# Chunked ridge attention and an fp4 feed-forward on one core: three passes against one, and two ways to invert the same small matrices

## The reference, cut to what matters

```python
G = Kc.T @ Kc + RIDGE_EPS * I            # 64 x 64
W = jnp.linalg.solve(G, Kc.T @ Vc)
U = U0                                   # first RANK = 8 unit vectors
for _ in range(POWER_K):                 # 2 rounds
    U, _ = jnp.linalg.qr(W @ U)
Wr = U @ (U.T @ W)
S_new = DECAY_ALPHA * S + Wr
out = SCALE * (Qc @ S_new)
```

```python
h = _layernorm(x) * (1 + ca) + sa
x = x + ga * attention(h)
h = _layernorm(x) * (1 + cb) + sb
x = x + gb * fp4_linear(silu(fp4_linear(h, w_gate)) * fp4_linear(h, w_up), w_down)
```

## Time and profile before

| what | value |
|---|---|
| runs | 1950.42, 1954.88, 1956.24 us |
| profiled execution, span from first to last instruction | 1955.5 us |
| DVE busy | 1637.0 us (84%) |
| PE busy | 1111.4 us (57%) |
| ACT busy | 796.1 us (41%) |
| POOL busy | 120.1 us (6%) |
| DMA, mean over the span | 38 GB/s |

### The profile page before, as it was taken

The page is one execution under the profiler, slowest core; times in us unless marked ns, Lnnn a source line. Parts: engine busy times, 40 slices in busy tenths (PEclk is TensorE's granted clock), DMA queues, the critical chain, the costliest instruction groups (busy, mean ns, idle before and its releaser), DMA issues. The chain is left out here.

```text
span 1955.5 us, 54893 instructions
## 1 busy us (share of the span) xinstructions
PE 1111.4 (57%) x21470; PEld 912.4 (47%) x21470; DVE 1637.0 (84%) x5229; ACT 796.1 (41%) x1499; POOL 120.1 (6%) x119
## 2 busy tenths in 40 slices
PE   2438201891662876776486867377407717347876
PEld 1325101851552863575485456277306616235554
DVE  6865799699999489999939999976998970399997
ACT  3645100652541553673354465255406404124342
POOL 3530000000000002000001100000201000200000
PEclk6659655695895688898669889758758959579998
DMA  2551000000000002100000200000121110411220
GB/s 91 173 182 57 27 0 0 15 29 12 3 3 1 4 3 81 35 4 3 2 4 24 81 2 4 2 3 4 61 78 43 39 39 2 132 51 57 66 64 28
DMA packets 58236, 73.85 MB, mean 38 GB/s; under 512 B 4512, under 2 KB 32880, under 8 KB 57984
## 3 DMA queue, kind: packets, MB, share of 16 engines
q1 hardware_dynamic: 57984, 70.38, 11.4%
HBM read 44.61 MB, written 25.76 MB: 36 GB/s over the span
## 5 line engine op out<-in xcount | busy, mean ns | idle before, releaser
L1500 DVE TENSOR_TENSOR a_blocks<-a_blocks,a_outer 128x384 f32<-128x384 f32 (+3 forms) x1024 | 455.3, 487 | 0.0
L1494 DVE TENSOR_TENSOR a_outer<-a_blocks,a_scaled 128x128 f32<-128x128 f32 (+3 forms) x1024 | 440.7, 492 | 2.0 <-DVE a_blocks L1528 1.3
L1150 ACT ACTIVATE a_pair<-a_bank 32x512 f32<-32x512 f32 (+1 forms) x352 | 207.2, 592 | 205.6 <-PE a_bank L932 126.5
L932 PE MATMUL a_bank<-a_ident,a_blocks 128*128 128x128 f32 x256 | 46.8, 367 | 366.7 <-DVE a_blocks L1510 366.7
L1150 ACT ACTIVATE a_work<-a_bank 32x512 f32<-32x512 f32 (+1 forms) x224 | 130.7, 589 | 294.5 <-PE a_bank L932 222.9
L932 PEld LDWEIGHTS a_bank<-a_ident,a_blocks 128*128 128x128 f32 x256 | 45.3, 214 | 368.3 <-DVE a_blocks L1510 197.8
L883 PE MATMUL a_bank<-a_wk,a_cg 128*128 128x512 f32 x256 | 123.6, 630 | 11.5 <-issue 11.5
L951 PE MATMUL a_bank<-a_work,a_gram 64*32 64x32 f32 (+1 forms) x4096 | 105.8, 220 | 17.9 <-issue 14.7
L951 PEld LDWEIGHTS a_bank<-a_work,a_gram 64*32 64x32 f32 (+1 forms) x4096 | 98.6, 135 | 23.4 <-issue 21.4
L1150 ACT ACTIVATE a_xb<-a_bank 128x512 f32<-128x512 f32 x112 | 63.4, 596 | 112.4 <-PE a_bank L1056 63.8
L1432 POOL TENSOR_TENSOR a_xc<-a_xc,a_ga 128x512 f32<-128x512 f32 x16 | 23.2, 1453 | 1358.2 <-ACTq L1155 1311.6
(11 more groups left out here) (212 smaller groups left out, 2625.5 us busy)
## 6 DMA issues: line engine op xcount, KB each, us to landing
f_x<-in_L_attn_x SPq DMA_DIRECT2D x16, 256.0 KB, 3.2
s_xnt<-f_xt SPq DMA_DIRECT2D x16, 256.0 KB, 2.1
s_c<-f_cm SPq DMA_DIRECT2D x16, 256.0 KB, 2.3
s_base<-f_base SPq DMA_DIRECT2D x16, 256.0 KB, 2.8
a_cg<-s_c SPq DMA_DIRECT2D x16, 256.0 KB, 2.7
a_cc<-s_c SPq DMA_DIRECT2D x16, 256.0 KB, 3.6
a_xnt<-s_xnt SPq DMA_DIRECT2D x16, 256.0 KB, 3.7
a_base_in<-s_base SPq DMA_DIRECT2D x16, 256.0 KB, 2.7
```

Of the source, the lines that this page charges most:

```text
L932: last = nc.tensor.transpose(bank[:, i * P:(i + 1) * P], rows_[:, :, 4 * jb + i], ident[:])
L1150: nc.scalar.activation(out, view, ACT.Copy, scale=scale).then_inc(emptied, 1)
L1494: made[a] = ch.inc(V.tensor_tensor(outer[a // KEPT], bcast(factor, 3, HB - a), bcast(scaled[:, :, a:HB], 2, KEPT), ALU.mult))
L1500: differences = ch.inc(V.tensor_tensor(strip, strip, outer[a // KEPT], ALU.subtract))
```

## The change

Nearly every part of the program is written anew.

- **One block.** The three passes become one `main_pass` without hardware loops; the code is written out. The moments and turned tokens of the first group stay in SBUF, the weights of the feed-forward too, and the fp4 input of the feed-forward is no longer stored and loaded.
- **Factors row by row.** `invert` is replaced by `factor`. It works out a triangular factor of the inverse, one row and column per step in 31 steps, then scales it with square roots that GpSimd makes in three parts (`roots`). The inverse itself is a product of two such factors, made by TensorE: `scale_rows` multiplies the factor with the other block, `squares` multiplies the result with itself.
- **The known corner.** The trailing corner of G is turned to one matrix per partition by a step of its own (`corner_extract`), and VectorE adds it to the turned product (in `schur` of VectorE).
- **Stages woven.** The steps are generators. `woven` interleaves two lists of steps on TensorE and ScalarE in proportion to their units: `output(g)` and `head(g+1)` with the gram stage of group g+2, `write(g-1)` with `assemble(g)`, and in the last group the feed-forward with `subspace`, `output` and `write`.
- **Gates on ScalarE.** The gates `ga` and `gb` are turned once and used as scales when ScalarE empties a bank; the residual is added by TensorE as one more matmul. GpSimd's combine and VectorE's `finish` go.
- **Smaller edits.** `apply_inverse` takes both heads of a pair in one matmul of 16 columns; `orthogonalise` needs one product fewer per vector and no longer waits for TensorE before its last scaling; the fp4 rounding has one operation fewer.

The core of the diff:

```diff
-                    for j in range(HB):
...
-                        for a in strips:
-                            factor = m[:, :, a:a + KEPT, j] if a < low else m[:, :, j, a:a + KEPT]
-                            made[a] = ch.inc(V.tensor_tensor(outer[a // KEPT], bcast(factor, 3, HB - a), bcast(scaled[:, :, a:HB], 2, KEPT), ALU.mult))
...
-                            strip = m[:, :, a:a + KEPT, a:HB]
-                            differences = ch.inc(V.tensor_tensor(strip, strip, outer[a // KEPT], ALU.subtract))
+                    for j in range(HB - 1):
+                        i, n_i = j + 1, HB - 1 - j
+                        row, rest = m[:, :, 0:j, j], m[:, :, 0:j, i:HB]
+                        ch.wait(inverse)
...
+                        weights = ch.inc(V.scalar_tensor_tensor(weight[:, :, 0:i], m[:, :, i, 0:i], -1.0, recip[:, :, 0:i], ALU.mult, ALU.mult))
+                        column = ch.inc(V.scalar_tensor_tensor(m[:, :, j, i:HB], m[:, :, i:HB, j], -1.0, bcast(recip[:, :, j], 2, n_i), ALU.mult, ALU.mult))
+                        ch.wait(weights)
+                        terms = area(0, n_i, i)
+                        known = ch.inc(V.tensor_tensor(terms, m[:, :, i:HB, 0:i], bcast(weight[:, :, 0:i], 2, n_i), ALU.mult))
+                        if j:
+                            ch.wait(column)
+                            step = area(2 * KEPT * KEPT, j, n_i)
+                            product = ch.inc(V.tensor_tensor(step, bcast(m[:, :, j, i:HB], 2, j), bcast(row, 3, n_i), ALU.mult))
+                        ch.wait(known)
+                        summed = ch.inc(V.tensor_reduce(total[:, :, 0:n_i], terms, op=ALU.add, axis=AX_X))
+                        if j:
+                            ch.wait(product)
+                            ch.inc(V.tensor_tensor(rest, rest, step, ALU.add))
+                        ch.wait(summed)
+                        ch.link(V.tensor_tensor(m[:, :, i:HB, i], m[:, :, i:HB, i], total[:, :, 0:n_i], ALU.add))
+                        inverse = pivot(i)
...
+                    dve.wait_ge(roots_ok, n * 3)
+                    V.tensor_tensor(m[:, :, 0:KEPT], m[:, :, 0:KEPT], bcast(root[:], 2, KEPT), ALU.mult)
...
+            for g in range(G - 1):
+                if g == 0:
+                    straight(e.assemble(g))
+                else:
+                    woven(e, (e.write(g - 1), WRITE_UNITS), (e.assemble(g), ASSEMBLE_UNITS))
+                straight(e.subspace(g))
+                straight(e.corner_extract(g + 1))
+                straight(e.lead_return(g + 1))
+                straight(e.schur(g + 1))
+                if g + 2 < G:
+                    woven(e, (chain(e.output(g), e.head(g + 1)), OUTPUT_UNITS + HEAD_UNITS), (feed(e, g + 2), FEED_UNITS))
```

More of the change, by code:

```diff
@@ new lines, in write, with straight, woven @@
+                    self.act.sem_inc(xnt_used, 1)
+                    yield
+        def straight(steps):
+            for _ in steps:
+                pass
+        orders = {}
+        def woven(e, *parts):
+            done, order = [0] * len(parts), []
+            live = list(range(len(parts)))
+            while live:
+                i = min(live, key=lambda k: (done[k] / parts[k][1], k))
+                at = e.u.n
+                try:
+                    next(parts[i][0])
+                except StopIteration:
+                    live.remove(i)
+                done[i] += e.u.n - at
+                order.append((i, e.u.n))
+            e.order.append(tuple(order))
+            assert orders.setdefault(len(e.order), e.order[-1]) == e.order[-1]
@@ new lines, in feed, with fronts, ffn, units @@
+        def feed(e, g):
+            yield from e.gram_stage(g)
+            yield from e.lead_extract(g)
+        def fronts(e, first, last):
+            for b in range(first, last):
+                yield from e.front(b)
+        def ffn(e, *steps):
+            for kind, b in steps:
+                yield from {"g": e.gate_up, "t": e.turn_hidden, "y": e.down, "n": e.tile_hat}[kind](b)
+        def units(steps):
+            return sum({"g": GATE_UNITS, "t": NW, "y": 2, "n": 0}[kind] for kind, b in steps)
```

1778 lines of the change are left out of this document (936 added, 842 removed).

## The result

The changed kernel takes **1326.65 us** (median of 4 runs, 1321.76 to 1328.19) against 1954.66 us (1950.42 to 1956.24) on the same chip: ratio 0.679, 95% interval 0.677 to 0.681. The profiled execution is the fastest of the four (1321.76 us) and has a span of 1319.9 us. The forecast was 1375 us, in a range of 1285 to 1480.

The account below looks back on a forecast made before the run. Eight VectorE inversions of 126 us were taken as half the 1955.5 us span. Start to 252 us, then group phases, each ended by its slower engine, to 993, then the last stage to 1375 us; range 1285 to 1480.

Parts of the forecast that it names:

- P2: Group phase: VectorE factors a leading corner, 80 us; TensorE's write, assembly and subspace end it at 98 (first group 78).
- P3: Group phase, 47 us: corner turning, lead_return and Schur stage on TensorE at the slow small-matmul rate, VectorE orthogonalising beside it.
- Factor, 77 us: One new triangular factor on VectorE: 77 us, bounds 65 to 95, with GpSimd's roots costed at nothing.
- slower than before: Rival: VectorE pays per element for short, strided, broadcast rows in the elimination; about 2030 us at 3.2 ns, chance 0.02.
- Start and first factors: Before the group cycle: corner 0 reaches VectorE at 119 us, Schur block 0 starts at 252.
- P1: Group phase: VectorE factors a Schur block, 79 us; TensorE's gram stage, output and head end it at 84.
- Cycle: One full group, from one Schur factor to the next: 84, 98 and 47 us; last Schur block done at 993.
- Last stage, 382 us: From the last Schur block at 993 us to the end at 1375, with the feed-forward covering the last group.
- Weaving fills nothing: Rival: each woven list takes the sum of its parts alone, 87 us more in all; 1462 us, chance 0.2.
- TensorE quicker: Rival: small matmuls keep 1.20 us for 64 records; P1 79, P2 82, P3 36; 1265 us, chance 0.13.
- The rule weighed: Tile-shape changes drain TensorE, estimated 0.17 us; about 370 interleaved pieces would give some 60 us more, about 1435; not adopted.
- the 392 us of the eight factors: VectorE time saved by eight shorter factors: 8 x 49 us.

Follow-up runs that it names:

- e3: Changed kernel without the product and last add on the inverse's earlier rows in each elimination step, 1e4 added to the diagonal; output not the reference's: 1283.91 us.
- e11: Control: the changed kernel itself, unedited, measured once more on the same chip as later runs: 1334.56 us, ratio 0.6825.
- e7: Changed kernel with one unread 128x512 matmul added ahead of each of the eight small-matmul stages of every Schur complement: 1341.36 us.
- e1: Changed kernel with weaving taken out of the loop over groups; output, feed, head, assembly and write each issued straight: 1374.47 us.
- e2: Changed kernel with the three weavings of the last group taken out, including those with the feed-forward: 1391.16 us.
- e4: Changed kernel with the reduction of the products made twice in every elimination step, its first result unread: 1424.16 us.
- e9: Changed kernel with the first 8 of 12 parts of write(2) issued beside the last Schur factor, only the last 4 woven with assembly: 1336.33 us.
- e13: Changed kernel with three unread 128x512 matmuls added ahead of each of the eight small-matmul stages of every Schur complement: 1357.60 us.

## Why the prediction was right, step by step

The forecast was 48 us above the median and 55 above the profiled span, and its main terms are those that the trace shows: the factor's length, phases that end by their slower side, and a feed-forward that covers the last group. Its waits are not: P2 was to keep VectorE waiting 18 us, twice, and keeps it 1.3 at most, and P3 was to keep it 16 us and keeps it 8 to 11.

- **Factor, 77 us.** Right: 77.7 from the operation on the diagonal to the hand-over, 2.98 us a step in mid-matrix (3.0 forecast). The price per element held for operations that the earlier trace rows did not show, and GpSimd's roots keep VectorE 0.17 us, as good as the nothing that I put. The rival *slower than before*, by such rows, is out.
- **Start and first factors.** Corner 0 at 110.9 (119 forecast), Schur block 0 at 254.7 (252), the first P2 over at 413.4 (409). The first is 8 us early, the fronts and the Schur stage behind it 11 late, and that the two nearly cancel is luck. Three of the 8 are a slip of the sum: 22 and four times 6.75 are 49, not 52.
- **P1, 84 us.** Right in kind (TensorE and VectorE nearly equal), too large: 78. TensorE's own sum is 77 (e3), where I had 83. An `apply_inverse` part takes 2.1 us instead of the 2.6 that I carried over from the earlier trace rows:

```profile
1001.37 1.09 PE L825 MATMUL a_bank<-a_pair,a_yz 128*16 128x64 f32 x64
1002.38 1.12 PE L840 MATMUL a_bank<-a_ident,a_xb 128*64 128x32 f32 x32
```

  Four parts are 2 us of the 6; the rest lies in `output`, `head` and the gram stage and was not split further.
- **P2, 98 us.** The term that failed most: 82.3 and 82.6 us (82.8 and 82.5 in e11). Write with assembly takes 48 us woven (532 to 580), where I had 58, and the subspace 34 instead of 40. I took the assembly at its 38 us and let its gaps hide only part of 7 us of new matmuls; alone it takes 35 us in the kernel after (332.5 to 367.4) and write some 20 to 22, and woven they lose 8 of their sum. Three of the 16 us too much are again a slip: `write` was 18 and 4 less 5, 17, where I put 20. The expected wait of 18 us before the orthogonalisation is 1.3.
- **P3, 47 us.** The slow rate, which I chose, is right (3.75 us for 128 records; the earlier trace rows have 1.92 for 64). From the basis (614.43) to the factor behind the adds (658.85) are 44.4. I had put all of the corner's turning, 6, on the path; it is issued ahead of the wait for the leading factor and lies beside it where TensorE is early, as in the first cycle. The reason for the slow rate I left open; the rival took the clock of 0.66 for it, and e7 shows that it isn't.
- **Cycle.** From one Schur factor to the next 204.5 and 205.2 us instead of 229: P1 6, P2 16 and P3 3 too large, twice. The last Schur block is done at 941.7, not 993, and these 51 us are nearly all of the 55 by which the forecast lies above the profiled span.
- **Last stage, 382 us.** 379. Write and assembly 49 (58), subspace with the gates 51 (50), orthogonalisation 30 (31), with TensorE standing 18.4 us (20):

```profile
1070.77 1.97 PE L868 MATMUL a_bank<-a_ident,a_basis 128*128 128x128 f32 x8 [18.38 <-DVE a_basis L1647]
```

  then 127 us with TensorE busy 117 (127, over 90%), and 121 behind it (116).
- **The rivals.** *Weaving fills nothing* is out by e1 and e2. Weaving is worth 40 to 48 us in the loop, where I had 48, and 57 to 65 in the last stage, where I had 39. *TensorE quicker* was right for P1 (79) and P2 (82) and wrong for P3 (36) and for the last stage, which it gave to VectorE; the result lies between it (1265) and the forecast.
- **The rule weighed.** The 1435 us did not come. The rule holds all the same, and I misread: a change of tile shape costs time, but inside the listed records, so that no gap shows it. The same piece of four records of 128x352 in the last stage, first between pieces of another tile shape, then between pieces of their own:

```profile
1002.38 1.12 PE L840 MATMUL a_bank<-a_ident,a_xb 128*64 128x32 f32 x32
1003.44 1.45 PE L622 MATMUL a_bank<-a_scaled,a_blocks 128*128 128x352 f32 x4
1004.82 1.12 PE L840 MATMUL a_bank<-a_ident,a_xb 128*64 128x32 f32 x32
...
1188.03 1.05 PE L926 MATMUL a_bank<-a_xb,a_xnt 128*128 128x128 f32 x8
1188.92 1.35 PE L622 MATMUL a_bank<-a_scaled,a_blocks 128*128 128x352 f32 x4
1190.11 1.02 PE L924 MATMUL a_bank<-a_work,a_ident 128*128 128x512 f32 x2
```

  From its start to the next piece's start it takes 1.38 us in the first place (1003.44 to 1004.82) and 1.19 in the second (1188.92 to 1190.11); with one neighbour of another shape it is 1.29 (1141.15 to 1142.44). So each side of a change costs 0.1 us and a change 0.2. The Trainium skill (TensorEngine Tiling (Array Packing), Key Properties) says that a change of tiling mode drains TensorE, and the trace agrees; its 0.2 us is near the 0.17 us of my estimate. What failed is the number of changes. In TensorE's order of time the tile shape changes about 310 times in the kernel after, 6 times fewer in e1 and 35 to 39 times fewer in e2: straight code changes it nearly as often, and weaving adds 41 to 45 changes, not 370, which is some 8 or 9 us (an estimate from these counts and 0.2 us). The changes of straight code were in my sum already, since the 3.70 us of the wide piece in the earlier trace rows were taken between pieces of another shape.
- **What isn't shown.** No run puts the old `invert` into the new kernel, so the 392 us of the eight factors are not measured as such. By the traces a factor went from 126 to 78 us; e4 made each 13.4 us longer, 107 in all, and 90 to 98 us of that arrived. The single block, the gates on ScalarE and the smaller edits have no run of their own.

## What to carry to other kernels

Weaving two streams pays by the waits of the one, not by the length of the other: price it by the gaps that a stage shows alone, and don't count on moving the filler elsewhere, which gained nothing here (e9). Once two engines are balanced to a microsecond, a shorter stage on one of them gains only where the other has less to do: a factor 15 us shorter, eight times, gave 43 to 51 us, and 13 us longer, eight times, cost 90 to 98. For long straight runs of small matmuls count instructions, not columns: they came at 15 ns each, and a long matmul of 1.1 us ahead of each 3.75 us stage cost nothing there (e7), while three made the stage 4.25 us (e13).

## What the runs showed of the hardware that I had not expected

- 128 small matmul records with their 128 weight loads take 3.75 us in a long straight run of them, at a granted clock of 0.63 as at 0.93, and 1.5 us of array time when long matmuls let the supply run ahead (e13). The stops of 1.1 to 1.8 us, one after every 127 or 128 matmul records, are marked as waits for nothing.
- The granted clock followed the work: one 128x512 matmul ahead of each stage took P3's from 0.63 (414:458 in e2 0.61, 614:656 above 0.63) to 0.93, without making P3 shorter. A low clock there is a companion of the stops and not their cause.
- A change of tile shape costs TensorE 0.2 us, 0.1 on either side, inside the listed records (1.38, 1.29 and 1.19 us for the same piece).
- Long VectorE operations in a chain start 0.06 to 0.1 us before the one in front is over by its record, so summed busy times overstate what their removal gives: 29.7 us busy, 15.2 us gained (e3; the short ones that are left also wait more for each other).
